# A batched transformer block on one core: the norm ahead of cross-attention on ScalarE in place of VectorE

## The reference

```python
x_norm = modulate(_ln(x), shift_a, scale_a)
... self-attention over x_norm
x = x + gate_a[:, None] * attn_out          # x1 in the kernel
q_c = _ln(x) @ W_qc + b_qc                  # _ln(x1): the norm that is changed
kv_c = _ln(context) @ W_kvc + b_kvc
... cross-attention, x = x + c_attn_out     # x2
x_norm2 = modulate(_ln(x), shift_m, scale_m)
h = jax.nn.gelu(x_norm2 @ W_mlp1 + b_mlp1) @ W_mlp2 + b_mlp2
x = x + gate_m[:, None] * h
```

## Time and profile before

| | |
|---|---|
| runs | 899.6, 901.58, 903.73 us; median 901.58 |
| profiled execution | 899.01 us, its span 897.2 us |
| granted TensorE clock, mean | 0.973 |
| PE busy | 836.8 us, 93% |
| DVE busy | 640.4 us, 71% |
| ACT busy | 495.8 us, 55% |
| POOL busy | 354.4 us, 40% |
| chain that ended last | PE 76%, DVE 13%, issue 4%, ACT 2%, POOL 2% |

### The profile page before, as it was taken

How to read it: one execution, slowest core, us unless ns; L and a number is a source line. 1 busy time by engine, 2 the same in 40 slices (tenths; PEclk the granted TensorE clock), 3 DMA queues, 4 the chain that set the end, 5 groups by cost and what they waited for, 6 DMA issues and landing times.

```text
span 897.2 us, 19234 instructions
## 1 busy us (share of the span) xinstructions
PE 836.8 (93%) x7088; PEld 636.3 (71%) x7088; DVE 640.4 (71%) x1370; ACT 495.8 (55%) x934; POOL 354.4 (40%) x400
## 2 busy tenths in 40 slices
PE   5888999999999999999999999999999999989877
PEld 5656667677777777777777777776777777667656
DVE  4767987878878786868877786868878787843420
ACT  2152567566564756566565757565665746554432
POOL 4453235253451725253442625253442623240312
PEclk9698999999999999999999999999999999989789
DMA  6442241323222332423222332423222322111101
GB/s 229 159 147 84 84 131 61 120 83 108 79 86 63 104 100 72 126 77 118 77 70 77 103 96 72 131 72 119 84 72 76 103 75 83 38 60 36 25 1 36
DMA packets 79784, 79.27 MB, mean 88 GB/s; under 512 B 12681, under 2 KB 74250, under 8 KB 79306
## 3 DMA queue, kind: packets, MB, share of 16 engines
q1 hardware_dynamic: 79402, 77.50, 27.2%
q10 hardware_dynamic: 288, 0.54, 0.2%
HBM read 22.82 MB, written 4.26 MB: 30 GB/s over the span
## 4 chain that ended last, share of the span: by engine, by line
PE 76%; DVE 13%; issue 4%; ACT 2%; POOL 2%; SPq 1%; DMA 1%; DVEq 0%; POOLq 0%; ACTq 0%
PE bank L673 19%; PE scan L762 13%; PE bank L706 12%; PE pv L719 12%; PE bank L697 7%; PE score L772 5%; PE bank L686 4%; PE bank L652 4%; DVE MX_x L1048 3%; DVE xn_y L938 2%; DVE MX_y L1048 1%; DVE stats_y L927 1%; DVE PN L971 1%; SPq L426 1%; DVE x L996 1%
## 5 line engine op out<-in xcount | busy, mean ns | idle before, releaser
L891 ACT ACTIVATE P<-score 128x512 f32<-128x512 f32 x512 | 286.0, 597 | 208.8 <-PE score L772 205.8
L1048 DVE TENSOR_REDUCE MX_x<-scan 128x2 fp32r<-128x512 f32 x256 | 166.6, 676 | 59.1 <-PE scan L762 58.8
L1048 DVE TENSOR_REDUCE MX_y<-scan 128x2 fp32r<-128x512 f32 x256 | 167.1, 679 | 41.4 <-PE scan L762 41.4
L673 PE MATMUL bank<-xT_y,W 128*128 128x256 f32 x960 | 134.9, 297 | 3.9 <-POOL xT_y L558 2.6
L673 PEld LDWEIGHTS bank<-xT_y,W 128*128 128x128 f32 x960 | 123.6, 198 | 11.8 <-issue 4.7
L706 PE MATMUL bank<-w_down,HH 128*128 128x256 f32 x512 | 127.6, 395 | 1.0 <-ACT HH L853 1.0
L762 PE MATMUL scan<-KS_x,QS_x 63*128 63x256 f32 x512 | 110.4, 327 | 10.3 <-DVE MX_x L1048 6.7
L772 PE MATMUL score<-QS_y,KS_y 64*128 64x256 f32 x512 | 107.3, 317 | 2.8 <-ACT P L891 2.7
L762 PE MATMUL scan<-KS_y,QS_y 63*128 63x256 f32 x512 | 103.0, 315 | 6.9 <-DVE MX_y L1048 5.5
L762 PEld LDWEIGHTS scan<-KS_y,QS_y 63*128 63x128 f32 x512 | 70.7, 187 | 53.9 <-issue 29.0
L706 PEld LDWEIGHTS bank<-w_down,HH 128*128 128x128 f32 x512 | 94.8, 194 | 19.1 <-ACT HH L853 1.7
(11 more groups left out here) (112 smaller groups left out, 1278.7 us busy)
## 6 DMA issues: line engine op xcount, KB each, us to landing
KS_x<-SK SPq DMA_DIRECT2D x96, 128.0 KB, 2.1
QS_x<-SQ_x SPq DMA_DIRECT2D x96, 128.0 KB, 2.1
KS_y<-SK SPq DMA_DIRECT2D x96, 128.0 KB, 2.6
QS_y<-SQ_y SPq DMA_DIRECT2D x96, 128.0 KB, 2.1
x_in<-in_x SPq DMA_DIRECT2D x16, 256.0 KB, 2.8
c_in<-in_ctx SPq DMA_DIRECT2D x16, 256.0 KB, 3.2
gate_a<-d_gate SPq DMA_DIRECT2D x16, 256.0 KB, 3.5
gate_m<-d_gate SPq DMA_DIRECT2D x16, 256.0 KB, 3.5
```

The costliest lines, as they stand in the source:

```text
L673: last = nc.tensor.matmul(to[:, i * N:(i + 1) * N], w[p][:, c, (blk + i) * 128:(blk + i + 1) * 128], xT[k][:, q, c, :], start=(n == 0), st ...
L891: nc.scalar.activation(P[:, s % 8, :, :].rearrange("p a n -> p (a n)"), score_bank[s % 2][:, :], ACT.Exp, scale=SCALE).then_inc(s_exp, 1)
L1048: nc.vector.tensor_reduce(MX[s1][:, half, col:col + NB], scan_bank[n % NSCAN][:, :].rearrange("p (a n) -> p a n", a=NB), AXIS.X, ALU.max, ...
```

## The change

VectorE's two-instruction norm of x1 is taken out. In its place VectorE makes one small product of 128 x 2, `shift` = -mean * rstd, at the same place of its plan (`shift_y`, slot 7; slot 6 at t = 15), and ScalarE makes `xn["y"]` = rstd * x1 + shift in two activations of 128 x 256 with a per-partition scale and a per-partition bias (`norm_y`). In ScalarE's plan the new task stands right ahead of its `T_y`: behind the exponential of slot 8 in most steps, at slot 3 for t = 1, slot 7 for t = 15, and at slot 8 ahead of the ups for t = 16. GpSimd's `root` gets one more wait, on `s_xn` of the batch before. PE's plan is not touched.

```diff
 ACT_PLAN = {
-          7), ("T_y", -1, 8), ("q_y", -1, 12), ("q_x", 1, 14), ("v_y", -1, 15)],
+          7), ("norm_y", -1, 8), ("T_y", -1, 8), ("q_y", -1, 12), ("q_x", 1, 14), ("v_y", -1, 15)],
...
-    "A1": [("T_x", 1, 0), ("v_x", 0, 3), ("k_x", 1, 3), ("T_y", -1, 3), ("q_y", -1, 6), ("q_x", 1, 15), ("v_y", -1,
-          15)],
+    "A1": [("T_x", 1, 0), ("v_x", 0, 3), ("k_x", 1, 3), ("norm_y", -1, 3), ("T_y", -1, 3), ("q_y", -1, 6), ("q_x",
+          1, 15), ("v_y", -1, 15)],
...
-    "AB-1": [("v_x", 0, 4), ("up0", -3, 6), ("up1", -3, 6), ("up2", -3, 6), ("up3", -3, 6), ("T_y", -1, 8), ("q_y",
-          -1, 13), ("v_y", -1, 15), ("T_c", 0, 15)],
+    "AB-1": [("v_x", 0, 4), ("up0", -3, 6), ("up1", -3, 6), ("up2", -3, 6), ("up3", -3, 6), ("norm_y", -1, 7),
+          ("T_y", -1, 8), ("q_y", -1, 13), ("v_y", -1, 15), ("T_c", 0, 15)],
...
+    "AB+0": [("T_m", -3, 4), ("norm_y", -1, 8), ("up0", -3, 9), ("up1", -3, 9), ("up2", -3, 9), ("up3", -3, 9),
...
 DVE_PLAN = {
-          5), ("stats_y", -1, 5), ("norm_y", -1, 7), ("k_x", 1, 8), ("T_y", -1, 8), ("max_x0", 0, 10), ("pt_y0", -2,
+          5), ("stats_y", -1, 5), ("shift_y", -1, 7), ("k_x", 1, 8), ("T_y", -1, 8), ("max_x0", 0, 10), ("pt_y0",
...
                 pool.wait_ge(s_ve[k], b + 1)
+                wait(pool, s_xn[k], b)
                 nc.gpsimd.tensor_tensor(rstd[k][:, :], var_eps[k][:, :], minus_half[:, :],
...
+            def norm_y(b):
+                act.wait_ge(s_shift, b + 1)
+                wait(act, s_xm["m"], b - 1)
+                for a in range(NB):
+                    last = nc.scalar.activation(xn["y"][:, a, :], x1[:, a, :], ACT.Identity,
+                                                bias=shift[:, a:a + 1], scale=rstd["y"][:, a:a + 1])
+                last.then_inc(s_xn["y"], 1)
...
-            def norm_y(b):
+            def shift_y(b):
                 dve.wait_ge(s_rstd["y"], b + 1)
-                wait(dve, s_xm["m"], b - 1)
-                for a in range(NB):
-                    last = nc.vector.tensor_scalar(xn["y"][:, a, :], x1[:, a, :], mv["y"][:, a, 0:1],
-                                                   rstd["y"][:, a:a + 1], ALU.subtract, ALU.mult)
-                last.then_inc(s_xn["y"], 1)
+                wait(dve, s_xn["y"], b)
+                nc.vector.scalar_tensor_tensor(out=shift[:, :], in0=mv["y"][:, :, 0], scalar=-1.0, in1=rstd["y"][:, :],
+                                               op0=ALU.mult, op1=ALU.mult).then_inc(s_shift, 1)
```

More of the change, by code:

```diff
@@ L92 @@
     "B0": [("q_x", 1, 7), ("T_c", 0, 7), ("k_y", 0, 13)],
-    "A1": [("T_x", 1, 0), ("v_x", 0, 3), ("k_x", 1, 3), ("T_y", -1, 3), ("q_y", -1, 6), ("q_x", 1, 15), ("v_y", -1,
-          15)],
+    "A1": [("T_x", 1, 0), ("v_x", 0, 3), ("k_x", 1, 3), ("norm_y", -1, 3), ("T_y", -1, 3), ("q_y", -1, 6), ("q_x",
+          1, 15), ("v_y", -1, 15)],
     "B1": [("T_c", 0, 8), ("k_y", 0, 14)],
-    "AB-1": [("v_x", 0, 4), ("up0", -3, 6), ("up1", -3, 6), ("up2", -3, 6), ("up3", -3, 6), ("T_y", -1, 8), ("q_y",
-          -1, 13), ("v_y", -1, 15), ("T_c", 0, 15)],
+    "AB-1": [("v_x", 0, 4), ("up0", -3, 6), ("up1", -3, 6), ("up2", -3, 6), ("up3", -3, 6), ("norm_y", -1, 7),
+          ("T_y", -1, 8), ("q_y", -1, 13), ("v_y", -1, 15), ("T_c", 0, 15)],
     "BB-1": [("k_y", 0, 11)],
-    "AB+0": [("T_m", -3, 4), ("up0", -3, 9), ("up1", -3, 9), ("up2", -3, 9), ("up3", -3, 9), ("T_y", -1, 9), ("q_y",
-          -1, 13), ("v_y", -1, 15)],
+    "AB+0": [("T_m", -3, 4), ("norm_y", -1, 8), ("up0", -3, 9), ("up1", -3, 9), ("up2", -3, 9), ("up3", -3, 9),
+          ("T_y", -1, 9), ("q_y", -1, 13), ("v_y", -1, 15)],
     "AB+1": [("T_m", -3, 1), ("up0", -3, 10), ("up1", -3, 10), ("up2", -3, 10), ("up3", -3, 10), ("T_m", -2, 15)],
@@ L118 @@
           ("pn_x0", 0, 9), ("po_x0", 0, 9), ("stats_x", 2, 11), ("k_y", 0, 13), ("pt_x1", 0, 14)],
-    "A1": [("pn_x1", -1, 2), ("po_x1", -1, 2), ("stats_c", 0, 6), ("out_x", -1, 6), ("stats_y", -1, 6), ("norm_y",
+    "A1": [("pn_x1", -1, 2), ("po_x1", -1, 2), ("stats_c", 0, 6), ("out_x", -1, 6), ("stats_y", -1, 6), ("shift_y",
           -1, 7), ("k_x", 1, 7), ("T_y", -1, 7), ("max_x0", 0, 9), ("q_y", -1, 11), ("q_x", 1, 13), ("max_x1", 0,
@@ L124 @@
     "AB-1": [("pt_x1", -1, 0), ("pn_x1", -1, 0), ("po_x1", -1, 3), ("max_y1", -2, 3), ("out_x", -1, 6), ("stats_y",
-          -1, 6), ("norm_y", -1, 6), ("max_x0", 0, 9), ("T_y", -1, 9), ("stats_c", 0, 12), ("pt_y0", -2, 13),
+          -1, 6), ("shift_y", -1, 6), ("max_x0", 0, 9), ("T_y", -1, 9), ("stats_c", 0, 12), ("pt_y0", -2, 13),
           ("q_y", -1, 13), ("pn_y0", -2, 14), ("po_y0", -2, 15), ("pt_y1", -2, 15), ("T_c", 0, 15), ("pn_y1", -2,
@@ L130 @@
     "AB+0": [("pn_x0", -1, 0), ("down1", -4, 1), ("pt_x1", -1, 1), ("max_y1", -2, 2), ("po_x0", -1, 2), ("pn_x1",
-          -1, 7), ("po_x1", -1, 7), ("out_x", -1, 7), ("stats_y", -1, 7), ("norm_y", -1, 7), ("T_y", -1, 9),
+          -1, 7), ("po_x1", -1, 7), ("out_x", -1, 7), ("stats_y", -1, 7), ("shift_y", -1, 7), ("T_y", -1, 9),
           ("pt_y0", -2, 9), ("q_y", -1, 10), ("pn_y0", -2, 10), ("po_y0", -2, 11), ("pt_y1", -2, 11), ("pn_y1", -2,
@@ L276, in build @@
         rstd = {k: sb(f"rstd_{k}", [128, NB]) for k in "xycm"}
+        shift = sb("shift", [128, NB])
         minus_half = sb("minus_half", [128, NB])
@@ L306, in build @@
         s_ident = sem("s_ident")
+        s_shift = sem("s_shift")
         s_ones = sem("s_ones")
@@ L868, in _ @@
                 **{f"up{u}": lambda b, u=u: up(u, b) for u in range(4)},
+                "norm_y": norm_y,
                 "T_y": lambda b: copied("T_y", "y", b),
@@ L1021, in _ @@
                 "out_y": out_y,
-                "norm_y": norm_y,
+                "shift_y": shift_y,
                 "stats_x": lambda b: stats_of("x", x_in[b % 2], b),
```

## The result

The changed kernel took 923.5 us as a median of four runs (917.6 to 925.9), the kernel before 902.1 (899.6 to 903.7). The ratio is 1.023, with a 95% interval of 1.017 to 1.029. Forecast were 932 us and a range of 913 to 943. The direction and the waits came as said; the falls of the clock were far fewer, one term was missing from the sum, and of the 30 us forecast 21 arrived.

The account below looks back on a forecast made before the run. The PE was taken as the bound, its wait at T_y moving everything. 899.0 us plus 16.9 of waits and 14.9 of clock falls gave 930.8 (933.4 from the median); forecast 932 us, range 913 to 943.

Parts of the forecast that it names:

- What bounds the kernel: PE, busy 93% of the span: a change to its wait at T_y moves its whole stream, with hardly any later absorption.
- The relief: VectorE loses two instructions per batch, 1.68 us; costed at nothing, since the PE hardly waits for the row maxima.
- The product: VectorE's 128 x 2 product: 166 ns, or held by POOL until about 460.5; hidden by ScalarE's queue in the steady part.
- 20 us or more: Sign on VectorE: its busy time should fall by this much without effect.
- POOL's additional wait: On POOL, a wait on something long done: some 0.05 us, with 0.4 us of cover, so free.
- ScalarE's pair: Two activations of 128 x 256 on ScalarE behind the exponential: 1.06 us, bounds 0.84 and 1.10.
- batches 2 to 13: Twelve steady batches, each with T_y later by 1.04 us: 12.5 us in all.
- batch 14: Norm between the exponentials of slots 7 and 8, behind four ups and a table load: +2.2 us (1.0 to 2.5).
- Everything else in the steady part is the PE running back to back: PE's steady part apart from the T_y and row-maxima waits: hardly any later wait to absorb a change at T_y.
- 11 falls over batches 1 to 14: TensorE clock falling to 1.2 GHz behind the new 2.0 us waits: 11 x 1.35 = 14.9 us, bounds 0 to 28.4.
- The first rival: Same waits at T_y but TensorE's clock holds, no falls: 917 us; chance 0.24.
- The other side: VectorE's maxima queue sets the PE's pace, so freeing 1.68 us per batch shortens the step: 888 us; chance 0.03.

Follow-up runs that it names:

- e4: Kernel before, with the gate_a load put ahead of the k_x stack in SyncE's plan for the steady steps: 897.45 us, ratio 0.997.
- e9: Changed kernel, with the gate_a load put ahead of the k_x stack in the steady steps: 924.0 us, ratio 1.027.
- e10: Kernel before, with three throwaway instructions of the norm's form on VectorE ahead of its norm, delaying the transposes: 914.0 us, ratio 1.016.
- e8: Changed kernel, with one throwaway activation of 128 x 256 on ScalarE ahead of each norm_y, lengthening the wait before T_y: 948.1 us, ratio 1.053.
- e2: Changed kernel, with VectorE also making the old two-instruction norm into a spare tile: 924.4 us, ratio 1.028.
- e1: Changed kernel, with fourteen throwaway matmuls on the PE in front of the transposes of T_y: 918.3 us, ratio 1.022.
- e7: Changed kernel, with ScalarE's norm_y behind k_x but ahead of the exponential of slot 8 in the steady steps: 918.8 us, ratio 1.020.
- e5: Kernel before, with POOL's x2_bias moved behind norm_c and the gate_a load ahead of the k_x stack: 887.9 us, ratio 0.986.

## Why the prediction came out as it did

**What bounds the kernel.** Right. e4 against e9, e10 and e8 show that a longer wait at `T_y` goes into the step one to one, with 1.04, 0.97 and 0.49 us. Nothing absorbs it.

**VectorE's side.** The relief was costed at nothing, and e2 measured 0.9 us for taking it back. The product was taken as held by POOL; it took 1.22 us beside POOL's L593 and 0.16 us where POOL was not in the way (batches 1 and 15). That it was hidden in the steady steps was right, and in batch 0 it was not hidden, as said. The Trainium skill, "SBUF — State Buffer" (section Who interferes with whom), says that a VectorE instruction with two SBUF inputs blocks against a GpSimd instruction that reads SBUF, for that one's whole length. The trace agrees: the product started at 421.11, 0.06 us behind L593, and ended at 422.33, 0.01 us behind it. The sign "20 us or more" did not follow from this: the product, held as the prediction itself took it, is busy for 17.5 us in all, against 25.0 us of the old norm, and shorter PN (36.1 to 30.6 us) brings the rest of the 12.6 us. POOL's additional wait was costed at some 0.05 us; from VectorE's aggregate to the start of rstd it is 0.35 us in both kernels, so it cost nothing.

**ScalarE's pair.** Taken as 1.06 us, it measured 1.09: a median of 602 ns each. The Trainium skill, "ScalarE: Activation LUTs" (What ACT_TABLE_LOAD costs), gives 0.833 ns per element, a base of 186 ns and some 93 ns for each per-partition operand; an estimate from these figures is 585 ns here, and the trace is 17 ns above it.

**The waits, batch by batch.**

| term | forecast, us | measured, us | from |
|---|---|---|---|
| batches 2 to 13 | +12.5 | +12.5 | 12 x 1.04, e9 against e4 |
| batch 1 | +1.5 | +1.6 | wait 2.01, was 0.45 |
| batch 14 | +2.2 | +2.4 | wait 2.38, was 0 |
| batch 0 | +0.7 | +0.4 | wait 2.44, was 2.02 |
| batch 15 | 0 | 0 | no wait in either |
| collisions of PN with x_bias and late query loads gone | 0 | -3.5 | 11 x 0.32, e4 |
| clock | +14.9 | +7.1 | an estimate, below |
| sum | +31.8 | +20.5 | medians: +21.4 |

In the changed kernel the transposes before and after the longer wait read:

```profile
372.89 0.66 PE L655 MATMUL bank<-ident,xn_y 128*128 128x128 f32 x4 [2.01 <-ACT xn_y L856]
...
423.90 0.66 PE L655 MATMUL bank<-ident,xn_y 128*128 128x128 f32 x4 [2.02 <-ACT xn_y L856]
```

a step of 51.01 us, and not 50.30 + 1.04.

**The first step that failed, a term left out: "Everything else in the steady part is the PE running back to back".** "I cost this gain at nothing" looked at VectorE's relief, and for that it was right. But the 2.4 us of waits for row maxima in the earlier trace rows were a clue that I set aside: they fell in some steps and not in others, and came from PN being held behind x_bias. I did not ask what a later `T_y` would do to the timing of two engines against each other. PN stands behind `T_y`, x_bias hangs on a DMA behind k_x, and the 1.04 us slid them apart. In the kernel before, x_bias started 6.90 us behind `T_y` at t = 5 and PN 7.15 us behind it; in the changed kernel, at t = 7, they stand at 6.12 and 7.14. A delayed PE also undoes a collision, and lets the late query loads of t = 9 and 13 land in time: 2.9 and 0.6 us in the other direction.

**The second, a term mis-sized: "11 falls over batches 1 to 14".** The price per fall was about right. Every execution lists its span and mean granted clock, so its time at 1.2 GHz is 2 x span x (1 - clock); over the 50 executions of the kernel before that ran beside the experiments, the span grows by 0.36 us per microsecond at the lower clock, where the forecast had 1.35 / 3.4 = 0.40. The count was wrong: the profiled execution had three falls behind the fourteen waits, and the mean time at 1.2 GHz went from 54.9 us in those 50 executions to 74.6 us in the four of the changed kernel, thus 19.7 x 0.36 = 7.1 us. I had taken the three stretches of the earlier trace rows as a rule, though in each of them the PE had idled more than once; a single 2.0 us wait amid dense work mostly passes. That such waits cause the falls at all is shown by e1 (filled: none) and e8 (2.5 us: eight of twelve).

The first rival, that the clock holds (917), was closer than the forecast by 2 us, and neither had it right: falls do come, but fewer. No error cancelled another here, since the clock term and the one left out both lay on the same side; that the range still held was owed to its taking in that rival. The Trainium skill, "TensorE: Matmul & The Clock Gate" (section Why this matters for your kernels), warns only of clearly longer gaps, and eleven of the fourteen waits of about 2 us did leave the clock up. The falls behind single waits of 1.65 us (three of twelve steady steps, e7) and 2.5 us (eight of twelve, e8) show that shorter ones can take it down too. The other side, VectorE as the true holder, is out by e2 and e10.

## What to carry to other kernels

Where one engine runs back to back, read the one wait it has and ask which queue ends it: moving work onto an idle engine costs what stands ahead of it in that engine's order, here k_x and an exponential, and what it takes longer there, and the source engine's relief buys nothing where the busy engine does not wait for it. Before moving work, look at what holds it up where it is. Half of this norm's time was a neighbour's instruction on POOL, and reordering that neighbour together with one DMA (e5) gained 1.4%, while the move lost 2.3%. And a delay slides engines and DMA queues against each other, so a pair of instructions that collides in some steps and not in others, or a load that only just lands in time, is a term of its own in the sum.

## What the runs showed of the hardware that was not expected

- A product of 128 x 2 on VectorE took 1.22 us when it started just after a POOL instruction of 1.27 us, and 0.16 us where no POOL instruction ran beside it.
- TensorE's clock fell to 1.2 GHz behind eight of twelve otherwise equal waits of 2.5 us, and behind only one or two of twelve at 2.0 us; behind these waits it stayed there for 3.4, 6.8 or 10.2 us. Fourteen throwaway matmuls in a 2.0 us wait kept it up.
- A load of the cross-attention's queries usually landed 2.1 us after its issue. In the thirteen traces 18 of these loads took over 3.5 us, and beside each of them a packet of 16 KB on the queue that the page calls "instruction" was under way for 0.9 to 1.9 us; of some 1090 loads that landed within 2.3 us, 83 had such a packet beside them (started from 0.5 us before the issue to 2 us after it). No run tested whether that packet is the cause.
